# Handing a quarter of the barrier additions from TensorE to VectorE in a two-layer graph kernel

## The reference, cut to what matters

```python
h = relu(layernorm(x))
qkv = h @ W_qkv + b_qkv                       # 8 heads of 16
scores = where(adj, q @ k.T / 4, -inf)        # per head, 512 x 512
x = x + softmax(scores) @ v @ W_out + b_out
h = relu(layernorm(x))
z_l, z_g, v = h @ Wl, h @ Wg, h @ Wv
A_l = cosine(z_l), A_g = exp(-|z_g - z_g'|^2 / 2)   # relu of the cosine; both without diagonal
K = 0.9 * rownorm(A_l * adj) + 0.1 * rownorm(A_g * adj)
x = x + K @ v @ Wo
```

## Time and profile before

| what | value |
|---|---|
| median of 3 runs | 874.0 us (873.55 to 875.01) |
| the profiled execution | 872.33 us, span 870.6 us |
| PE busy | 814.5 us, 94% |
| DVE busy | 674.6 us, 77% |
| ACT busy | 544.3 us, 63% |
| POOL busy | 532.0 us, 61% |

### The profile page before, as it was taken

The page is one execution under the profiler, slowest core; times in us unless marked ns, Lnnn a source line. Parts: engine busy times, 40 slices in busy tenths (PEclk is TensorE's granted clock), DMA queues, the critical chain, the costliest instruction groups (busy, mean ns, idle before and its releaser), DMA issues.

```text
span 870.6 us, 15444 instructions
## 1 busy us (share of the span) xinstructions
PE 814.5 (94%) x4860; PEld 467.4 (54%) x4860; DVE 674.6 (77%) x1950; ACT 544.3 (63%) x1230; POOL 532.0 (61%) x701
## 2 busy tenths in 40 slices
PE   3869899999999999999999999999999999999986
PEld 2223245646564655656565564656556565646466
DVE  5666669798887969788796978878797888878266
ACT  5427485765758485665848566574957657474832
POOL 4266766675857567585756658575665757474611
PEclk9899899999999999999999999999999999999999
DMA  3350505032140503113050402304050221300000
GB/s 94 100 138 3 141 1 141 1 102 53 43 111 1 152 2 114 41 58 96 5 148 2 141 13 78 76 22 132 2 153 2 85 69 36 106 2 13 13 1 25
DMA packets 49840, 54.75 MB, mean 63 GB/s; under 512 B 7264, under 2 KB 43616, under 8 KB 49760
## 3 DMA queue, kind: packets, MB, share of 16 engines
q1 hardware_dynamic: 49760, 53.76, 22.5%
HBM read 30.28 MB, written 23.07 MB: 61 GB/s over the span
## 4 chain that ended last, share of the span: by engine, by line
PE 54%; DVE 16%; POOL 11%; issue 7%; ACT 6%; DMA 3%; SPq 2%; POOLq 0%; DVEq 0%; ACTq 0%
PE adj L722 12%; PE pv L708 9%; PE score L680 7%; PE turned L694 7%; DVE scrap L955 6%; PE adj L717 6%; PE work L740 4%; PE turned L693 4%; POOL probs_t L547 3%; DVE adj_cos L974 3%; DVE adj_rbf L988 3%; DVE rbf_arg L983 2%; PE work L717 2%; POOL v_cos L632 2%; POOL v_cos L629 2%
## 5 line engine op out<-in xcount | busy, mean ns | idle before, releaser
L547 POOL TENSOR_TENSOR probs_t<-probs_t,keep_t 128x512 int32<-128x512 int32 x256 | 322.4, 1280 | 213.4 <-ACT probs_t L1126 213.1
L955 DVE CUSTOM_DVE_ANT_0 scrap<-score,mask_add 128x512 f32<-128x512 f32 x512 | 340.0, 683 | 67.6 <-PE score L680 65.3
L1126 ACT ACTIVATE probs_t<-turned 128x512 f32<-128x512 f32 x512 | 296.2, 601 | 110.5 <-PE turned L694 105.1
L680 PE MATMUL score<-qk_rows 96*128 96x512 bf16 x512 | 198.9, 388 | 12.1 <-DMA qk_rows<-k_dram 6.0
L694 PE MATMUL turned<-qk_rows 99*128 99x512 bf16 x512 | 196.2, 383 | 9.7 <-ACT probs_t L1126 8.8
L708 PE MATMUL pv<-probs_t,v_cols 128*32 128x512 f32 x1024 | 138.1, 612 | 0.0
L680 PEld LDWEIGHTS score<-qk_rows 96*128 96x128 bf16 x512 | 49.9, 98 | 119.8 <-DVE neg_max L955 55.2
L693 PE MATMUL turned<-bar_t,ident_b 128*128 128x512 bf16 x256 | 98.0, 383 | 0.7 <-ACT probs_t L1126 0.7
L694 PEld LDWEIGHTS turned<-qk_rows 99*128 99x128 bf16 x512 | 50.6, 99 | 54.7 <-ACT probs_t L1126 18.3
L1160 ACT ACTIVATE rbf_exp<-rbf_arg,rbf_bias 128x512 f32<-128x512 f32 x64 | 46.2, 722 | 34.7 <-DVE rbf_arg L983 32.8
L722 PEld LDWEIGHTS adj<-v_cos,adj_cos 128*128 128x128 f32 x480 | 62.8, 191 | 8.8 <-DVE out_sb L1011 0.6
(11 more groups left out here) (159 smaller groups left out, 1221.9 us busy)
## 6 DMA issues: line engine op xcount, KB each, us to landing
q_dram<-split SPq DMA_DIRECT2D x96, 128.0 KB
qk_rows<-q_dram SPq DMA_DIRECT2D x32, 384.0 KB, 4.3
k_dram<-split SPq DMA_DIRECT2D x48, 128.0 KB
qk_rows<-k_dram SPq DMA_DIRECT2D x32, 192.0 KB, 4.8
x_sb<-in_x_dram SPq DMA_DIRECT2D x16, 256.0 KB, 4.2
qk_rows<-k_dram SPq DMA_DIRECT2D x32, 128.0 KB, 4.9
out_dram<-out_sb SPq DMA_DIRECT2D x15, 256.0 KB, 2.5
qk_rows<-k_dram SPq DMA_DIRECT2D x32, 64.0 KB, 5.2
```

What stands on the lines that cost most here:

```text
L547: pool.tensor_tensor(tile, tile, keep_t[:, w // HG % T, :], ALU.mult).then_inc(probs_masked.sem, 1)
L680: pe.matmul(score_bank[u % 2][:, :], qk_rows[0:ROWS, b % 2, 0, h, t * P:(t + 1) * P], qk_rows[0:ROWS, b % 2, 1, h, :], start=True, stop=Tr ...
L955: dve.tensor_tensor_reduce(scrap[:, u % 2, :], score_bank[u % 2][:, :], mask_add[:, u % T, :], -1.0, 3.0e38, ALU.add, ALU.min, neg_max[:, ...
L1126: act.activation(probs_t[:, k % 4, w % HG, :], turned_bank[w % 2][:, :], ACT.Exp, scale=SCALE).then_inc(probs_ready.sem, 1)
```

## The change

`MASK_BY_PE` shrinks to (3,), and `MASK_BY_DVE` = (2,) is new. For these tiles (8 of 32) TensorE no longer adds the barrier. VectorE adds it while it moves the tile from the turned bank to the new SBUF buffer `barred`, and ScalarE takes the exponential from there. TensorE waits for VectorE (`barred_ready`) where it refills such a bank. `scrap` becomes bfloat16. And `AT` is rewritten in many places by one or a few slots; the places of the DMA stages move by up to 16.

```diff
-MASK_BY_PE = (2, 3)
+MASK_BY_PE = (3,)
+MASK_BY_DVE = (2,)
...
-    "pv": (28, 32, 36, 40, 44, 48, 52, 56), "y": (54, 59), "yT": (60,), "attn": (62,), "h2T": (66,),
+    "pv": (28, 32, 36, 40, 44, 48, 52, 56), "y": (55, 59), "yT": (61,), "attn": (62,), "h2T": (67,),
...
-    "cos": (81, 83, 84, 90), "mix_cos": (92, 95, 96, 97), "mix_rbf": (94, 95, 96, 97),
-    "ln_scale": (-28,), "hT_copy": (-26,), "q_hi": (-24,), "k_hi": (-22,), "max_copy": (17, 31),
-    "pv_copy": (42, 56), "yT_copy": (60,), "ln2_scale": (64,), "h2T_hi": (66,), "z_copy": (70, 71, 72, 74),
-    "z_sums": (71, 72, 74, 75), "zgT_hi": (75,), "col_copy": (77,), "zlT_hi": (79,), "rbf_exp": (82, 83, 86, 90),
-    "ln_moments": (-36,), "hT_split": (-26,), "q_rest": (-24,), "k_rest": (-21,), "v_add": (-13,),
+    "cos": (81, 83, 84, 89), "mix_cos": (92, 95, 96, 97), "mix_rbf": (94, 95, 96, 99),
+    "ln_scale": (-28,), "hT_copy": (-26,), "q_hi": (-24,), "k_hi": (-22,), "max_copy": (18, 31),
+    "pv_copy": (42, 56), "yT_copy": (60,), "ln2_scale": (65,), "h2T_hi": (66,), "z_copy": (69, 71, 72, 74),
+    "z_sums": (70, 72, 74, 75), "zgT_hi": (75,), "col_copy": (77,), "zlT_hi": (79,), "rbf_exp": (81, 83, 85, 88),
+    "ln_moments": (-36,), "hT_split": (-25,), "q_rest": (-24,), "k_rest": (-21,), "v_add": (-13,),
...
-    "zgT_lo": (76,), "zlT_lo": (79,), "rbf_read": (80, 83, 85, 87), "cos_read": (81, 83, 85, 90),
-    "rbf_mask": (83, 84, 88, 92), "out": (94, 96, 97, 101),
-    "ln_rstd": (-32,), "q_split": (-20,), "k_split": (-12,), "x_biased": (-13,), "ln2_rstd": (62,),
+    "zgT_lo": (76,), "zlT_lo": (79,), "rbf_read": (79, 83, 85, 88), "cos_read": (81, 83, 85, 90),
+    "rbf_mask": (83, 84, 88, 92), "out": (93, 96, 97, 101),
+    "ln_rstd": (-32,), "q_split": (-22,), "k_split": (-12,), "x_biased": (-14,), "ln2_rstd": (62,),
...
-    "qk_store": (-12,), "rows": (-6, -4), "x_next": (-9,), "max_load": (-2, 29), "store": (95,),
+    "qk_store": (-25,), "rows": (-11, -3), "x_next": (-18,), "max_load": (7, 31), "store": (98,),
...
-        scrap = sb("scrap", [P, 2, N])
+        scrap = sb("scrap", [P, 2, N], BF16)
+        barred = sb("barred", [P, N])
...
+                if (w - 2) % SLOTS in by_dve:
+                    reached(pe, barred_ready, *((b, by_dve.index(w - 2) + 1) if w >= 2 else (b - 1, len(by_dve))))
+                else:
+                    reached(pe, probs_ready, b, w - 1)
...
+                if hit := tile_due(s, LAG):
+                    b, w = hit
+                    if w in by_dve:
+                        reached(dve, turned_filled, b, w + 1)
...
+                        dve.tensor_tensor(barred[:, :], turned_bank[w % 2][:, :], bar_t[:, w // HG % T, :],
+                                          ALU.add).then_inc(barred_ready.sem, 1)
...
+                    src = turned_bank[w % 2]
+                    if w in by_dve:
+                        reached(act, barred_ready, b, by_dve.index(w) + 1)
+                        src = barred
+                    act.activation(probs_t[:, k % 4, w % HG, :], src[:, :], ACT.Exp,
```

More of the change, by code:

```diff
@@ L107, in graph_blocks @@
     by_pe = [w for w in range(SLOTS) if w % HG in MASK_BY_PE]
-    by_pool = [w for w in range(SLOTS) if w % HG not in MASK_BY_PE]
+    by_dve = [w for w in range(SLOTS) if w % HG in MASK_BY_DVE]
+    by_pool = [w for w in range(SLOTS) if w not in by_pe and w not in by_dve]
     def slots_of(name, batch):
@@ L295, in graph_blocks @@
         turned_filled = signal("turned_filled", SLOTS)
+        barred_ready = signal("barred_ready", len(by_dve))
         probs_ready = signal("probs_ready", SLOTS)
@@ L690, in turned_scores @@
                     reached(pe, max_loaded[g], b)
-                reached(pe, probs_ready, b, w - 1)
+                if (w - 2) % SLOTS in by_dve:
+                    reached(pe, barred_ready, *((b, by_dve.index(w - 2) + 1) if w >= 2 else (b - 1, len(by_dve))))
+                else:
+                    reached(pe, probs_ready, b, w - 1)
                 if w in by_pe:
@@ L701, in attend @@
                 reached(pe, probs_masked, b, sum(w < ends for w in by_pool))
-                if by_pe:
-                    reached(pe, probs_ready, b, 1 + max(w for w in by_pe if w < ends))
+                reached(pe, probs_ready, b, 1 + max(w for w in by_pe + by_dve if w < ends))
                 if j == 0:
@@ L874, in _ @@
                         reached(pe, probs_ready, b)
+                        reached(pe, barred_ready, b)
                     split_product(z_bank(b, t)[:, 0:3 * D],
@@ L958, in _ @@
                                              ).then_inc(max_ready.sem, 1)
+                if hit := tile_due(s, LAG):
+                    b, w = hit
+                    if w in by_dve:
+                        reached(dve, turned_filled, b, w + 1)
+                        if w >= HG:
+                            reached(dve, probs_ready, b, w - HG + 1)
+                        else:
+                            reached(dve, probs_ready, b - 1, w - HG + 1 + SLOTS)
+                        dve.tensor_tensor(barred[:, :], turned_bank[w % 2][:, :], bar_t[:, w // HG % T, :],
+                                          ALU.add).then_inc(barred_ready.sem, 1)
                 if (hit := due(s, "z_sums")) and hit[0] == B - 1:
@@ L1125, in _ @@
                         reached(act, pv_filled, b, k - 3)
-                    act.activation(probs_t[:, k % 4, w % HG, :], turned_bank[w % 2][:, :], ACT.Exp,
+                    src = turned_bank[w % 2]
[3 more added lines that the diff above has]
+                    act.activation(probs_t[:, k % 4, w % HG, :], src[:, :], ACT.Exp,
                                    scale=SCALE).then_inc(probs_ready.sem, 1)
```

## The result

The changed kernel takes **871.9 us** (median of 10 runs, 871.39 to 873.12), the kernel before, run beside it, 874.1 us (10 runs). The ratio is 0.9976, with a 95% interval of 0.9968 to 0.9985: faster by 2.2 us, 0.24%. The forecast was 866 us, 0.9% faster. The sign holds and the size does not. The profiled execution has a span of 869.7 us, where the kernel before has 870.6.

A forecast was written before the change was run, and what follows sets the result against it. A period of 50.13 us was taken as bound by three stretches: TensorE's, ScalarE's, then GpSimd's and VectorE's. -0.50 a period over fifteen periods, +0.8 and -0.9 gave -7.6, hence 866 us; own range 858 to 873, 8 in 10 851 to 884.

The forecast's parts named there:

- three stretches: Each period: TensorE's until `max_turn` at 457.87, ScalarE's until 471.4, then GpSimd's and VectorE's until `rbf` 3 at 491.
- -(0.44 + 0.5) + 0.34 + 0.10: Period sum: barrier matmuls saved in TensorE's and ScalarE's stretches, less late maxima and slower SBUF exponentials; -0.50 us.
- the 0.5: Barrier matmuls of slots 35, 7 and 11, beside ScalarE's stretch: 0.66 saved for TensorE, 0.5 taken as usable in ScalarE's pauses.
- 0.5 of room: Slack found for `h2T`, moved from slot 34 to 35, should the second layer norm be delayed: 0.5 us.
- my 0.34: Slots 23 to 31: VectorE's additions make maxima of slots 25 and 26 late for TensorE by 0.1 and 0.24.
- VectorE waits for GpSimd later anyway. Net 0: Slot 19's addition (0.60) in the third stretch costs nothing; `rbf_read` 0 (0.60) also moves from slot 16 to 15.
- third stretch gets shorter: Rival: the first `rbf_mask` runs without being held by GpSimd; -1.5 us a period, 851 us, chance 0.22.
- ScalarE waits for the addition, taken as 0: Slots 3, 7, 11: the 0.68 addition fits into ScalarE's lag, cost 0, other end 2.0 a period; slot 15 also 0.
- VectorE the bound: Rival: uncovered additions between GpSimd's stretch and `h2T` delay the second layer norm; +1.0 us a period, 889 us, chance 0.24.
- the 0.5 named as the sign for it: Sign of a wrong prediction: `h2T` starts more than 0.5 us later after `rbf` 3 than the earlier 19.85.
- Start and end: One-time terms: +0.8 us at the start through later `max_load` on SyncE, -0.9 at the end through moved `h2T`.
- nothing moves: Rival: TensorE's saving goes into waits for VectorE and ScalarE's stretch; 874 us, between 872.3 and 875.7, chance 0.11.

The follow-up runs named there:

- y_slot22: The changed kernel with the first `y` moved back to slot 22, ahead of `rbf` 3: 873.1 us, ratio 0.9982 to the kernel before.
- leave_19: The changed kernel without the addition in slot 19, that tile left unmasked: 857.5 us, period 48.83.
- leave_3_7: The changed kernel without the additions in slots 3 and 7, those two tiles left unmasked: 871.4 us, period 50.00.
- leave_11_15: The changed kernel without the additions in slots 11 and 15, those two tiles left unmasked: 873.4 us, period 50.07.
- bias_leave_23_31: The changed kernel with `x_biased` in slot 5 and the additions of slots 23, 27 and 31 left out, those tiles unmasked: 857.8 us, period 48.90.
- pe19: The changed kernel with slot 19's barrier added by TensorE again and the other seven by VectorE: 871.9 us, period 50.04.
- before_bias_early: The kernel before with GpSimd's `x_biased` alone moved from slot 19 to slot 5: 864.7 us, period 49.40.
- bias_early: The changed kernel with GpSimd's `x_biased` moved from slot 18 to slot 5, where GpSimd waits: 857.8 us, period 48.93.

## Why the prediction was wrong in size

Point by point, by its own steps.

- **What bounds the kernel.** Right: three stretches, `rbf` 3 waits for `rbf_read` 2 in both kernels, and `rbf_mask` is held by GpSimd in both. The chain of the changed kernel leaves TensorE earlier, at 462.2 with the copy of h2T, stays on ScalarE until 475.9 and then on VectorE until 491.26. It does not pass through GpSimd's list, as the chain before did from 471.56: GpSimd shows in it only as the length of `rbf_mask`.

```profile
485.77 1.38 DVE adj_rbf L1008
...
490.53 0.69 DVE rbf_arg L1003
491.26 0.96 PE adj L725 x3
```

- **The step that failed: the terms -(0.44 + 0.5) + 0.34 + 0.10 of the sum.** Those of TensorE's stretch (-0.44 + 0.34) measured +0.08. Those of ScalarE's (-0.5 + 0.10) measured -0.16. Together -0.08 instead of -0.50, and the period moved by -0.09.
- **The bigger miss is the 0.5.** I let ScalarE use all its pauses. One of them did go (0.30 before q), but the move of h2T behind slot 35 opened one of 0.38 at 462.21. The "0.5 of room" that I gave that move was TensorE's; ScalarE had none.
- **The smaller miss is TensorE's stretch.** Slot 28 starts 5.47 after `rbf` 3 instead of 5.25, +0.22 where the sum had -0.22 + 0.34 = +0.12; from there to `max_turn` it is -0.14 instead of -0.22. For slot 28 the sum put the move of the first `y` at nothing without a word: 0.44 of TensorE's work went from slot 22, ahead of the wait at `rbf` 3, to slot 23 behind it. 0.44 less the barrier matmul of slot 27 is the +0.22. `y_slot22` shows that VectorE's lateness, my 0.34, is as long by itself, 0.44 (5.47 against 5.25 - 0.22 = 5.03). What the stretch would gain without both was not run.
- **Third stretch, "VectorE waits for GpSimd later anyway. Net 0".** The outcome is near it (19.44 before, 19.43 after) and the reason is wrong, so the agreement is luck. The hold is not a fixed end that absorbs what comes before it; it goes by the instruction that GpSimd is in when `rbf_mask` comes. Before, `rbf_mask` came 0.13 after `x_biased` had begun (485.18 against 485.05), after the change 0.38 after the next instruction had begun (485.69 against 485.31), and both waited that one out. Without slot 19's addition it would have been in time: `leave_19`, -1.22 a period. So slot 19's addition costs 1.22 in this table, the largest single term of the change, and the rival "third stretch gets shorter" (851 us) was one addition away: 857.5.
- **ScalarE waits for the addition, taken as 0.** Right for the new table: its exponentials from `barred` in slots 3, 7 and 11 start without a pause, and `leave_3_7` gives 0.05 a period, `leave_11_15` and `bias_leave_23_31` nothing. It does wait in slots 23, 27, 15 and 19 (0.67, 1.96, 0.63 and 1.23), which makes up most of the 89.0 us of the page, and they cost nothing: `leave_11_15`, `bias_leave_23_31` and `pe19` take them away without a gain. The 0 is right only with `hT_split` behind the addition. With the old table the additions lost 2.35 a period in all, more than the 2.0 named as the other end.
- **The addition is not held by GpSimd.** Right: L977 beside GpSimd's list takes 0.68. The rule of the Trainium skill (SBUF — State Buffer, SBUF: two separate sides), that a VectorE instruction with two SBUF inputs and a GpSimd one that reads SBUF exclude each other, agrees with the rows shown: L1008 is held up to 1.79, L977 and L1003 with a bank as one input are not.
- **ScalarE from SBUF.** 637 - 596 = 41 ns, the 0.04 that I had estimated from the 52 cycles of the Trainium skill (VectorE: DVE Perf Modes, the section on the TRN2 errata). The trace agrees.
- **VectorE the bound.** Did not come. Its wait in slot 33 fell from 1.97 to 0.56, so the three additions ahead of it were covered, and h2T came 20.36 after `rbf` 3 instead of 19.85, 0.51 later and just past the 0.5 named as the sign for it. That sign misled: h2T follows TensorE's own eight matmuls of `mix_rbf` 3 without a pause, which the new table puts ahead of it.
- **Start and end.** The first period began 0.94 later (140.00 to 140.94; forecast +0.8), but not by the path that I named: the DMAs of `max_load` start at 46.61 instead of 46.44, 0.17 later and not 0.6 to 1.1. The agreement is luck, and where the 0.94 comes from was not traced. From the last `rbf` 3 of the table (batch 14) to the end of the span it is 0.2 less, forecast -0.9; why is not traced either. The sum: twelve regular periods brought -1.10, the two shorter ones behind them -0.54, so 0.94 - 1.10 - 0.54 - 0.2 = -0.9 of span, as measured.
- **The nearest rival in number is "nothing moves" (872.3 to 875.7).** It said that TensorE's saving goes into waits for VectorE and ScalarE's stretch, and slots 27 and 28 and the pause of 0.38 are of that kind. It did not have what holds the third stretch.

What the change is worth beside an early `x_biased` is 0.47 a period. Of this 0.22 is seen at the end of the first `rbf_mask` (45.43 to 45.21). The rest lies at the period's end. Timelines of TensorE there, `before_bias_early`, then `bias_early`:

```profile
486.38 0.38 PE L693 MATMUL turned<-bar_t,ident_b 128*128 128x512 bf16 x1
486.60 0.38 PE L694 MATMUL turned<-qk_rows 99*128 99x512 bf16 x1
486.63 1.05 PE L717 MATMUL adj<-zgT_parts 128*128 128x512 f32 x3
```

```profile
482.29 0.98 PE L725 MATMUL adj<-zgT_parts 128*128 128x512 f32 x3 [0.25 <-DVE rbf_arg L1003]
```

With `x_biased` early, the kernel before starts `rbf` 3 without a pause: TensorE's own list, slot 23's barrier matmul (0.22) in it, is what ends the period, and the expectation had this as its middle case. The changed kernel has no such matmul there and waits for VectorE. That this matmul makes up the rest of the 0.47 fits in size and was not run by itself.

## What to carry to other kernels

Where one engine holds another, ask not how long the hold is but which instruction it hangs on and how far the held one arrives from that instruction's start: 0.2 us of arrival was worth 1.2 us a period here, and a large saving elsewhere nothing. When a tile passes through two engines' in-order lists, check the order of each pair of hand-overs; one exchange cost 1.64 us a period, nearly the 1.76 that TensorE was relieved of. Where undoing a move brings nothing, look for a second list that is as long. And the cheapest move was the one that the change did not make: taking an instruction with slack out of the engine that holds (`bias_early`, 857.8 us, 1.8% below the kernel before and 1.6% below the changed one).

## What the runs showed of the hardware

Two things. VectorE's `rbf_mask` and GpSimd's instructions take turns at instruction boundaries: in all eight kernels `rbf_mask` ended 0.54 to 0.56 after the end of the GpSimd instruction under way at its arrival, whether that was the integer mask (L552), the float32 addition (L620) or a cast (L577, L582), and GpSimd's next instruction was stretched in return, whichever it was (L552 1.74 for 1.28, L584 1.50 for 1.16, L582 1.07 for 0.61). The second `rbf_mask` of the changed kernel follows the same rule: it ends at 488.27 + 1.13 = 489.40, 0.55 after L584 (487.69 + 1.16 = 488.85). And the held time appears as the instruction's duration and not as a wait, so no view of waits names it: the same line takes 0.69 at the median and up to 1.79.
